# Layer norm inside a feed-forward phase: variance and inverse deviation computed on a whole 128x512 tile instead of on 128x4 columns

## The reference, cut to what matters

```
x = x + 0.5 * ffn(layernorm(x))
x = x + attention(layernorm(x))
x = x + 0.5 * ffn(layernorm(x))

layernorm(x) = (x - mean) / sqrt(var + 1e-5)        # over the 512 features
ffn(y):  prev = y of the token before (0 for the first of a sequence)
         xr = mu_r*y + (1-mu_r)*prev ; xk = mu_k*y + (1-mu_k)*prev
         out = sigmoid(xr @ W_r) * (square(relu(xk @ W_k)) @ W_v)
```

## Time and profile before

| what | value |
|---|---|
| median of 3 runs | 3391.86 us (3388.17 to 3393.8) |
| the profiled execution | 3392.48 us |
| its span (first to last instruction) | 3390.5 us |
| granted PE clock, mean share of full | 0.974 |
| PE busy | 3186.6 us (94%) |
| DVE busy | 2794.9 us (82%) |
| ACT busy | 1537.9 us (45%) |
| POOL busy | 1296.8 us (38%) |

### The profile page before, as it was taken

One profiled execution on the slowest core, in us unless ns is written; L12 is line 12 of the kernel. 1 busy time (PEld: TensorE's weight loads), 2 busy tenths in 40 slices (PEclk: granted clock), 3 DMA queues, 4 the chain that ended last, 5 costly groups with the idle time before them and its releaser, 6 DMA issues. The chain is left out here.

```text
span 3390.5 us, 189736 instructions
## 1 busy us (share of the span) xinstructions
PE 3186.6 (94%) x83236; PEld 2718.0 (80%) x83236; DVE 2794.9 (82%) x4862; ACT 1537.9 (45%) x2316; POOL 1296.8 (38%) x1195
## 2 busy tenths in 40 slices
PE   7999999799999999958999999999996987999999
PEld 5888888577776777748999999999995765888887
DVE  7787877889898988957999999999997857777875
ACT  4555554577767676741221122112213324555554
POOL 1232232200000000006887888888774421232322
PEclk9999999899999999988999999999997998999999
DMA  2222121333232333246777777777765773122221
GB/s 112 87 80 106 74 111 64 124 101 104 91 115 82 112 91 102 79 131 155 201 200 199 199 200 200 200 201 200 199 184 170 224 219 122 74 96 89 78 108 62
DMA packets 486566, 453.05 MB, mean 134 GB/s; under 512 B 55504, under 2 KB 448848, under 8 KB 467280
## 3 DMA queue, kind: packets, MB, share of 16 engines
q1 hardware_dynamic: 483632, 449.50, 43.9%
q10 hardware_dynamic: 2848, 2.56, 0.3%
HBM read 331.33 MB, written 120.60 MB: 133 GB/s over the span
## 5 line engine op out<-in xcount | busy, mean ns | idle before, releaser
L861 DVE SCALAR_TENSOR_TENSOR ain_conv<-ain_padded,ain_taps,ain_conv 128x512 f32<-128x512 f32 x576 | 447.8, 777 | 20.4
L381 POOL TENSOR_TENSOR ffn_out<-ffn_gate,ffn_xres 128x512 f32<-128x512 f32 x128 | 164.4, 1317 | 757.4 <-DVE ffn_gate L285 757.1
L1562 ACT ACTIVATE rec_u<-rec_ps_end 128x256 f32<-128x256 f32 x128 | 49.2, 384 | 631.7 <-PE rec_ps_end L1614 631.7
L942 POOL TENSOR_TENSOR ain_half<-ain_sq 128x1024 f32<-128x1024 f32 x15 | 41.6, 2775 | 700.9 <-ACT ain_sq L959 700.9
L1330 POOL TENSOR_TENSOR rec_d_norm<-rec_dmat,rec_early 128x512 f32<-128x512 f32 x128 | 162.8, 1272 | 173.8 <-DVE rec_dmat L1412 173.8
L46 PE MATMUL ffn_ring<-ffn_mixrh,ffn_wrh 128*128 128x512 f32 x512 | 202.0, 395 | 10.9 <-DVE ffn_mixrl L337 10.9
L46 PE MATMUL ffn_ring<-ffn_mixkh,ffn_wkh 128*128 128x512 f32 x512 | 205.8, 402 | 6.5 <-DVE ffn_mixkl L211 6.5
L46 PE MATMUL ffn_ring<-ffn_mixkh,ffn_wkl 128*128 128x512 f32 x512 | 203.2, 397 | 0.0
L46 PE MATMUL ffn_ring<-ffn_mixrh,ffn_wrl 128*128 128x512 f32 x512 | 203.2, 397 | 0.0
L46 PE MATMUL ffn_ring<-ffn_mixrl,ffn_wrh 128*128 128x512 f32 x512 | 202.5, 395 | 0.0
L46 PE MATMUL ffn_ring<-ffn_act_h,ffn_wvh 128*128 128x512 f32 x512 | 201.7, 394 | 0.0
(11 more groups left out here) (255 smaller groups left out, 9878.8 us busy)
## 6 DMA issues: line engine op xcount, KB each, us to landing
rec_early<-coeffs SPq DMA_DIRECT2D x512, 128.0 KB, 3.0
streams<-ain_buf SPq DMA_DIRECT2D x48, 1024.0 KB, 5.1
rec_qkv<-streams SPq DMA_DIRECT2D x126, 384.0 KB, 3.4
rec_qk_pe<-streams SPq DMA_DIRECT2D x127, 256.0 KB, 3.4
rec_late<-coeffs SPq DMA_DIRECT2D x504, 64.0 KB, 2.3
ffn_xres<-in_x SPq DMA_DIRECT2D x16, 1024.0 KB, 6.6
ffn_x<-x SPq DMA_DIRECT2D x16, 1024.0 KB, 8.3
gate<-ain_gate SPq DMA_DIRECT2D x16, 1024.0 KB, 3.9
```

The lines of the kernel that those rows point to most:

```text
L381: added = nc.gpsimd.tensor_tensor(out[:, m, :], gate[:, m, :], xres[:, m, :], ALU.add)
L861: nc.vector.scalar_tensor_tensor(out=out[:], in0=pad[:, n:n + TOK], scalar=taps[:, u // KT, u % KT, n:n + 1], in1=out[:], op0=ALU.mult, op ...
L942: nc.gpsimd.tensor_tensor(half2[:], sq[:, 0:2, :], sq[:, 2:4, :], ALU.add).then_inc(halved2, 1)
L1562: nc.scalar.activation(u[:], ps_end[:, :, 1, :], ACT.Copy).then_inc(u_ready, 1)
```

## The change

`var` now multiplies the rounded high part and the low part of `sum2` by the 128x128 matrix `mean_r` (all 1/512), two matmuls of 128x512 into `ps_rstd`; each partition then holds the variance of each token, so nothing has to be spread. For that ACT rounds `sum2` (new `squares_round`, placed after the third sigmoid) and POOL subtracts the rounded from the full value (new last step of `squares`). ACT takes the root of the whole 128x512 in PSUM in place, with epsilon as its bias, and DVE inverts the 128x512 in PSUM in place (new `inverse_deviation`). The products of `spread_rstd` leave the slots, as do the five small DVE instructions of `deviations`. `act_rest` piece 1 moves ahead of `differ`. The first tile of a phase keeps the old way.

```diff
         def _(dve):
+            nc.vector.memset(eps[:], LN_EPS)
...
+            def inverse_deviation(t):
+                dve.wait_ge(std_ready, t + 1)
+                nc.vector.reciprocal(ps_rstd[:], ps_rstd[:]).then_inc(spread, 1)
+
...
                 if ahead:
-                    deviations(t + 1)
+                    inverse_deviation(t + 1)
                 if ahead == "norm":
                     normalise_next()
                     ahead = 0
                 if ahead:
                     normalise(t + 1)
                 act_rest(t, 0)
+                act_rest(t, 1)
                 if ahead:
                     differ(t + 1)
-                act_rest(t, 1)
                 if ahead:
                     mixes(t + 1, "r", 0)
...
         def squares(t):                      # POOL
                 nc.gpsimd.tensor_tensor(sum2[:], half2[:, 0, :], half2[:, 1, :], ALU.add).then_inc(summed2, 1)
+                pool.wait_ge(sq_high, t)
+                nc.gpsimd.tensor_tensor(sum2_l[:], sum2[:], sum2_h[:].bitcast(F32), ALU.subtract).then_inc(sq_split, 1)
...
+            def squares_round(t):            # ACT
+                act.wait_ge(summed2, t)
+                nc.scalar.activation(sum2_h[:], sum2[:], ACT.Copy).then_inc(sq_high, 1)
+
             def deviation(t):
-                act.wait_ge(var_copied, t + 1)
-                nc.scalar.activation(std_tok[:], var_tok[:], ACT.Sqrt).then_inc(std_ready, 1)
+                act.wait_ge(var_done, t + 1)
+                nc.scalar.activation(ps_rstd[:], ps_rstd[:], ACT.Sqrt, bias=eps[:]).then_inc(std_ready, 1)
...
                 for m in range(3):
                     gates(t, m)
+                if more:
+                    squares_round(t + 1)
                 gates(t, 3)
                 if more:
                     deviation(t + 1)
...
             def var(t):                      # PE
-                pe.wait_ge(summed2, t)
-                for j in range(KT):
-                    last = nc.tensor.matmul(ps_mean[:, j:j + 1], sum2[:, j * P:(j + 1) * P], mean_w[:, 0:1], start=(j == 0),
-                                            stop=True, skip_group_check=True)
-                last.then_inc(var_done, 1)
+                pe.wait_ge(sq_split, t)
+                nc.tensor.matmul(ps_rstd[:], mean_r[:], sum2_h[:], start=True, stop=False)
+                nc.tensor.matmul(ps_rstd[:], mean_r[:], sum2_l[:], start=False, stop=True).then_inc(var_done, 1)
...
                 project(t, "k", 1, 1, k_done)
-                if more:
-                    spread_rstd(t + 1)
                 for m in range(2, KT):
```

More of the change, by code:

```diff
@@ L93, in ffn_phase @@
         sum_h, sum_l = sb("sum_h", [P, TOK], F32R), sb("sum_l", [P, TOK], F32R)
+        sum2_h, sum2_l, eps = sb("sum2_h", [P, TOK], F32R), sb("sum2_l", [P, TOK], F32R), sb("eps", [P, 1])
         mean_r, ones_r = sb("mean_r", [P, P], F32R), sb("ones_r", [P, P], F32R)
@@ L111, in ffn_phase @@
         v_used, out_ready = sem("v_used"), sem("out_ready")
+        sq_high, sq_split = sem("sq_high"), sem("sq_split")
         sum_high, sum_split, rstd_high, rstd_low = sem("sum_high"), sem("sum_split"), sem("rstd_high"), sem("rstd_low")
@@ L211, in mix_rest, with deviations @@
                 nc.vector.tensor_tensor(mix_l[n][:], mix[n][:], mix_h[n][:].bitcast(F32), ALU.subtract).then_inc(mix_low, 1)
-            def deviations(t, ps_var=ps_mean):
+            def inverse_deviation(t):
+                dve.wait_ge(std_ready, t + 1)
+                nc.vector.reciprocal(ps_rstd[:], ps_rstd[:]).then_inc(spread, 1)
+            def deviations(t):
                 dve.wait_ge(var_done, t + 1)
-                nc.vector.tensor_scalar_add(var_tok[:], ps_var[:, 0:KT], LN_EPS).then_inc(var_copied, 1)
+                nc.vector.tensor_scalar_add(var_tok[:], ps_rstd[:, 0:KT], LN_EPS).then_inc(var_copied, 1)
                 dve.wait_ge(std_ready, t + 1)
@@ L345, in _ @@
             dve.wait_ge(ident_step, 2)
-            deviations(0, ps_rstd)
+            deviations(0)
             weight_low("r", 0)
@@ L396, in square, with first_deviation @@
                 nc.scalar.activation(diff[:], xc[:], ACT.Square).then_inc(squared, 1)
+            def first_deviation():
+                act.wait_ge(var_copied, 1)
+                nc.scalar.activation(std_tok[:], var_tok[:], ACT.Sqrt).then_inc(std_ready, 1)
+            def squares_round(t):
+                act.wait_ge(summed2, t)
+                nc.scalar.activation(sum2_h[:], sum2[:], ACT.Copy).then_inc(sq_high, 1)
             def deviation(t):
-                act.wait_ge(var_copied, t + 1)
-                nc.scalar.activation(std_tok[:], var_tok[:], ACT.Sqrt).then_inc(std_ready, 1)
+                act.wait_ge(var_done, t + 1)
+                nc.scalar.activation(ps_rstd[:], ps_rstd[:], ACT.Sqrt, bias=eps[:]).then_inc(std_ready, 1)
             def high(t, n, nth):
@@ L472, in _ @@
             first_squares()
-            deviation(0)
+            first_deviation()
             weight_high("k")
```

## The result

The changed kernel takes 3420.1 us (median; 3413.9 to 3421.8), the kernel before 3390.6 in the same session, 29.5 us less. The forecast was 3422. The profiled execution took 3421.64, its span 3419.6.

A forecast was written before the change was run, and what follows sets the result against it. PE was taken to bound the kernel at 34.80 us a tile; the lengthened ring of 35.80 would replace it, adding 15.6 us in ffn2 and 14.6 in ffn1, +30.2 in all: 3422 us. Own range 3416 to 3439, stated range 3401 to 3442.

The forecast's parts named there:

- PE is the bound and 1.5 to 1.9 us from the next limit: Feed-forward tiles before: PE busy 34.80 of 34.80 us; the ring through four engines has 1.5 to 1.9 us to spare.
- PE needs 34.01: PE's time a tile after the change: 34.80 less 0.79 us for eight small `var` matmuls removed.
- the 0.12 that might have gone besides: The 12 matmuls after `var` take 2.87 us instead of 2.75; that excess on PE might go too.
- The ring: Path through DVE, ACT, POOL and PE from one normalisation (N) to the next: 28.62 + 7.18 = 35.80 us a tile.
- weight load, two matmuls and the way to the reader: Ring link on PE, from the weight load to the root's start: 0.96 us, priced from the spread's rows.
- The sum: Total growth over both feed-forward phases: ffn2 +15.6 and ffn1 +14.6, together +30.2 us, with tiles at +1.00.
- The ends: ffn2's first N +2.6 us, ffn1's +1.05; after the last N, PE saves 0.95 and 0.47, less stalls of 0.3 to 0.4 in ffn2.
- PE's wait: PE idle before `var` 1.5 to 2 us a tile, plus a stall of 0.3 for the last `act_l` pieces.
- The fast reciprocal: Rival, chance 0.06: reciprocal in PSUM as fast as other DVE work, ring 33.0 us, PE the bound, 3371 us.
- The tables: Rival, chance 0.05: rounding needs an extra table load on ACT, or a load costs more; root delayed, +0.8 a tile, 3446.
- PE's clock: Rival, chance 0.10: waits at `var` lower PE's clock, some +0.5 us a tile at worst, 3436.
- A shorter ring: Rival, chance 0.05: overlapping waits make the ring 1 us shorter than its links, no change, 3392.

The follow-up runs named there:

- Runs 2 and 3: Kernel before with one, then two, spare 128x512 POOL additions ahead of the sum of squares; 3398.0 us (ratio 1.0007) and 3427.1 us (1.0097).
- run 1: Changed kernel with the 128x512 reciprocal replaced by an addition of zero in PSUM, output not the reference's; 3374.4 us, ratio 0.9939 to the kernel before.
- run 10: Changed kernel with only `act_rest` pieces 2 and 3 moved ahead of mixes r; 3434.1 us, ratio 1.0119 to the kernel before.
- run 4: Changed kernel with the variance as one full-precision product of `sum2`, without rounding and subtraction; 3388.9 us, ratio 0.9986 to the kernel before.
- runs 7 and 10: Run 7: changed kernel with x loaded one tile further ahead and `sums` moved ahead of the reciprocal; 3403.5 us, ratio 1.0019. Run 10: see its line.
- run 9: Changed kernel with x loaded earlier, `sums` ahead of the reciprocal, last `act_l` pieces ahead of mixes, `sum_rest` earlier, mixes k split around `mix_rest` r; 3378.6 us, ratio 0.9958.

## Why the prediction was right

**PE is the bound and 1.5 to 1.9 us from the next limit**: right. Runs 2 and 3 measure 1.6 to 1.7. **PE needs 34.01**: right, 33.99 in run 1, which also shows that the 0.12 that might have gone besides did not.

**The ring**: right in its mechanism and in nearly all its terms: to the end of `sum2` 28.54 for 28.62; reciprocal 3.37 for 3.35; subtraction 1.27 for 1.29; rounding 0.63 for 0.63. Mis-sized was the term "weight load, two matmuls and the way to the reader", 0.96 with a hand-off of 0.06: the rows after give 0.83 for both, 0.19 less. The spread's row counted from a weight load that stood ahead of its matmul; in the new kernel 0.06 lie between the subtraction's end (3111.95) and the first matmul, and 0.77 from there to the root. The load (3056.43) stood 0.23 ahead of its matmul. The root took 0.66 instead of 0.60. Its row, L1017, has no bias vector among its inputs, which the price overlooked; in the kernel before an activation from PSUM with one takes 0.68:

```profile
L976 ACT ACTIVATE ain_padded<-ain_ps_ring,ain_bias 128x512 f32<-128x512 f32 x192 | 130.8, 681 | 15.5 <-PE ain_ps_ring L46 15.3
```

That speaks for the bias and not for the writing of PSUM, but no run separates the two. The other links took 0.05 less together, and N to the end of `sum2` 0.08 less. So the ring came out at 35.54 where 35.80 was predicted.

**The sum.** A tile of +0.78 instead of +1.00, just below the +0.8 to +1.6 that the prediction gave as its own bounds, accounts for 28 x 0.22 = 6.2 of the difference between +30.2 and +24.1. The ends were right: the first N of ffn2 lies 55.9 behind the start of its phase instead of 53.4, +2.5 for +2.6, and from the last N to the end it is 53.8 instead of 54.7, -0.9 for -1.0. In ffn1 the first N moved by 1.4 (predicted 1.05), and from its last N (542.8 before, 555.0 now) to the phase's end it is 56.3 for 56.9, -0.6 for -0.4. So the mechanism was right, and the growth of the tile was set 0.22 us too high. That the total still came within 2 us of the forecast is in part luck: it owes 5 us to the middle phases, which no step predicted. With the 24.1 us alone it would be 3416.6, at the lower end of the prediction's own range.

**PE's wait** was forecast at 1.5 to 2 and is 0.9 ahead of `var` plus 0.2 at `act_l` (0.3 forecast) as the profile counts idle time, or 1.13 and 0.46 by the starts of the matmuls. The figure was too high even by the prediction's own ring: 35.80 less 34.01 is 1.79 for both waits together.

**The rivals.** The fast reciprocal fell by its row (3.37 for 512 columns in PSUM, 3.35 in SBUF); run 1 shows what it would have given, 3374 where the prediction had 3371. The tables fell: ACT loads two in a tile, as before, the load ends 0.4 us ahead of the root, and the root starts 0.05 behind the second matmul's end. The drain of about 1380 ns that the Trainium skill counts for a switch ("ScalarE: Activation LUTs", What ACT_TABLE_LOAD costs) isn't there: the load of 3111.11 starts behind the sigmoid that began at 3110.51 and took 0.58. PE's clock stayed at 1.00, in this tile and over the whole of 2868 to 3366 us, in spite of an idle microsecond a tile. The rival was not empty, though: run 10, with longer waits, has one tile in which the clock fell. A shorter ring was true by a quarter of a microsecond, not by the whole one.

## What to carry to other kernels

Work taken from the engine that bounds is worth no more than the slack of the next ring, so sum that ring's links before cutting: here 0.8 us were taken from PE, and 2.4 added to a ring that had some 1.65 to spare (33.15 us before, 34.80 less 1.65; 35.54 after). A ring through several engines shows in no share of busy time, and the profile's chain can name a load instead; sum it from one tile's timelines and test its slack with a spare operation, which costs one run. Once a ring binds, move what it doesn't need into the idle time ahead of its slow link, expect a second and a third limit close behind, and keep an edit by the tile length that it gives, not by the wait that it removes.

## What was not expected of the hardware

- The reciprocal on DVE takes 3.37 us for 128x512 in PSUM, 3.35 in SBUF: 6.6 ns a column, where an addition at the same place takes 0.70 (run 1).
- A one-product variance in full precision takes 1.02 us on PE (run 4). The two rounded products, 0.50 and 0.39, overlap: from the start of the first to the end of the second it is 0.72 us (3112.01 to 3112.73).
- POOL and DVE slow each other down, and in more than one way: POOL's four additions take 5.07 or 7.26 us, DVE's 128x2048 subtraction beside them 3.39 or 2.28, and POOL's subtraction of 128x512 takes 1.27 alone and 1.49 beside DVE's sums. With the last tile left aside, the long kind (7.26) comes six times each in runs 7 and 10, three times in the changed kernel and never in the kernel before or in run 9; which tile it falls on follows from nothing that these runs show. What it costs depends on the ring: 0.77 us a tile in run 7, 0.2 in run 10.
- An idle time of PE of 1.85 us was followed by a clock at the lower level once in run 10, at a cost of 1.6 us, and once it was not.
